# Block attention with the values and the softmax sums on four column tiles of TensorE, and its affine part on GpSimd

## The reference, cut to what matters

```python
q = split_heads(x @ Wq)          # 16 heads of 8 features
k = split_heads(x @ Wk)
v = split_heads(x @ Wv)
scores = jnp.einsum('bhqd,bhkd->bhqk', q, k) / jnp.sqrt(jnp.float32(HD))
attn_w = jax.nn.softmax(scores, axis=-1)
ctx = jnp.einsum('bhqk,bhkd->bhqd', attn_w, v)
ctx = ctx.transpose(0, 2, 1, 3).reshape(b, s, d)
attn_out = ctx @ Wo + bo
out1 = _layernorm(x + attn_out, ln1_g, ln1_b)
```

## Time and profile before

| | |
|---|---|
| median of three runs | 1562.96 us (1562.08 to 1563.18) |
| profiled execution, its own time | 1561.37 us |
| span of the profiled execution | 1559.6 us |
| PE busy | 1352.5 us (87%) |
| DVE busy | 845.7 us (54%) |
| ACT busy | 710.9 us (46%) |
| POOL busy | 146.7 us (9%) |
| the stage's first and last record | 1111.1 us and 1286.7 us |

### The profile page before, as it was taken

The page is one execution under the profiler, slowest core; times in us unless marked ns, Lnnn a source line. Parts: engine busy times, 40 slices in busy tenths (PEclk is TensorE's granted clock), DMA queues, the critical chain, the costliest instruction groups (busy, mean ns, idle before and its releaser), DMA issues. The chain is left out here.

```text
span 1559.6 us, 26943 instructions
## 1 busy us (share of the span) xinstructions
PE 1352.5 (87%) x8843; PEld 1045.2 (67%) x8843; DVE 845.7 (54%) x2280; ACT 710.9 (46%) x1593; POOL 146.7 (9%) x256
## 2 busy tenths in 40 slices
PE   6766799999996899689999997984699987999995
PEld 5642477777775487578888886973477764766664
DVE  4549777777763554645555553346687762122224
ACT  4331676776762302245555552442355542333343
POOL 1010000000001000000000002005244421000000
PEclk9869899999996999889999997995699987999998
DMA  8000000000000000000000004002000000000000
GB/s 335 1 1 0 1 1 1 1 1 2 1 1 1 1 1 0 1 1 1 2 1 2 1 1 115 8 1 108 1 1 1 0 1 1 1 1 1 1 1 28
DMA packets 6427, 24.52 MB, mean 16 GB/s; under 512 B 797, under 2 KB 1311, under 8 KB 5418
## 3 DMA queue, kind: packets, MB, share of 16 engines
q1 hardware_dynamic: 6314, 23.03, 4.3%
HBM read 21.98 MB, written 1.05 MB: 15 GB/s over the span
## 5 line engine op out<-in xcount | busy, mean ns | idle before, releaser
L1317 DVE SCALAR_TENSOR_TENSOR XN<-bank,gate,XN 128x128 f32<-128x128 f32 x256 | 89.8, 351 | 224.8 <-PE bank L1281 222.2
L1297 ACT ACTIVATE e_hidden<-bank,small 128x512 f32<-128x512 f32 x152 | 104.4, 687 | 214.6 <-PE bank L1269 214.5
L767 PE MATMUL bank<-a_va,a_pT 128*128 128x65 f32 x1024 | 129.4, 269 | 0.8 <-ACT a_pT L933 0.5
L1281 PEld LDWEIGHTS bank<-attention_weights,e_hidden 128*128 128x128 f32 x1024 | 119.2, 192 | 14.8 <-issue 14.8
L767 PEld LDWEIGHTS bank<-a_va,a_pT 128*128 128x128 f32 x1024 | 124.4, 192 | 2.3 <-ACT a_pT L933 0.8
L1019 DVE TENSOR_REDUCE a_mx<-bank 128x4 f32<-128x512 f32 x128 | 87.8, 686 | 64.9 <-PE bank L807 64.4
L1269 PE MATMUL bank<-XNT,attention_weights 128*128 128x512 f32 x256 | 121.2, 606 | 1.2 <-PEq L541 1.2
L1281 PE MATMUL bank<-attention_weights,e_hidden 128*128 128x128 f32 x1024 | 119.3, 275 | 0.0
L933 ACT ACTIVATE a_pT<-bank 128x512 f32<-128x512 f32 x128 | 76.6, 599 | 41.8 <-PE bank L840 41.8
L1027 DVE TENSOR_TENSOR a_shifted<-bank,a_mx 128x512 f32<-128x512 f32 x128 | 88.3, 690 | 3.4
L1912 PEld LDWEIGHTS bank<-blk_va,blk_pT 128*128 128x128 f32 x512 | 64.5, 194 | 33.5 <-issue 21.9
(11 more groups left out here) (353 smaller groups left out, 2646.3 us busy)
## 6 DMA issues: line engine op xcount, KB each, us to landing
attention_weights<-in_a SPq DMA_DIRECT2D x2, 2048.0 KB, 11.7
mod_ring<-in_mod_weights SPq DMA_DIRECT2D x4, 576.0 KB
ctx_both<-in_ctx SPq DMA_DIRECT2D x1, 2048.0 KB, 9.2
attention_weights<-in_up SPq DMA_DIRECT2D x1, 2048.0 KB, 8.2
attention_weights<-in_down SPq DMA_DIRECT2D x1, 2048.0 KB, 12.7
down<-in_down SPq DMA_DIRECT2D x1, 1536.0 KB, 18.2
down<-in_mod_weights SPq DMA_DIRECT2D x2, 576.0 KB
X<-in_x SPq DMA_DIRECT2D x4, 256.0 KB, 3.9
```

Source lines behind the costliest of these rows:

```text
L767: last = pe.matmul(value_bank[:, j * (W + 1):(j + 1) * (W + 1)], pT[:, i.slot(2), j * 128:(j + 1) * 128], va[:, p, g // 2 * 8 + 2 * j + g ...
L1281: last = pe.matmul(down_bank[j][:, 0:width], layer[0:rows, f, j * 128:(j + 1) * 128], down(g, f), start=f == 0, stop=f == NB - 1)
L1297: act.activation(hidden[0:rows, p, f, :], up_bank_of(i, f)[0:rows, :], function, bias=up_bias(g, f)).then_inc(hidden_ready, 1)
L1317: dve.scalar_tensor_tensor(out=total, in0=down_bank[j][:, e * D:(e + 1) * D], scalar=gate_column(k, 4 * q + j, g * per_group + e), in1=tot ...
```

## The change

Nine things change in `stage_block_attention`, and nothing outside it.

1. The values are computed turned. The weights are now 32 columns of `va` and the moving operand is `pT` of one head, 128 columns. Each of the four matmuls of an item lies on another column tile of the array (`tile_position=(0, 32 * c)`), and writes 32 partitions of one bank. `va` has a stride of 40 per head with zeros between, and the window that is loaded moves with the group, so that each item adds its four heads' rows in the right place: the bank accumulates over a batch's four items.
2. The softmax sums are four more such matmuls, with a matrix of ones and zeros as the weights, into a second bank.
3. A group of heads is now every fourth head (`own`).
4. VectorE's reciprocal covers 128 columns instead of 16, and its product is already the turned output `oT`. The transposition of line 1903 and ScalarE's copy of line 1974 go.
5. There is one value bank where there were two, so a batch's first values wait for the batch before (`o_normed`).
6. Scaling, shifting and the copy to `out1` move from VectorE to GpSimd, with the new lag `AFFINE`, behind `BLOCKS` in GpSimd's body.
7. `ADD`, `NORMALISE`, `TURN_OUT` and `KEEP` have a later lag by one, one, one and three.
8. The turned output lies in the projection's bank, so that `TURN_OUT` waits for `qkv_kept`, and a projection for `out_kept`.
9. All four programs are written out (`rolled=False`), and GpSimd clears all of `va` and `ones` first.

```diff
 
-    PROJECT, KEEP_QKV, BLOCKS, SCORE, EXP, TURN_P, VALUES, NORM_O, TURN_O, OUT, ADD, NORMALISE, KEEP, TURN_OUT = \
-        0, 1, 4, 3, 5, 5, 6, 6, 7, 7, 7, 8, 9, 10
+    PROJECT, KEEP_QKV, BLOCKS, SCORE, EXP, TURN_P, VALUES, NORM_O, OUT, ADD, NORMALISE, AFFINE, TURN_OUT, KEEP = \
+        0, 1, 4, 3, 5, 5, 6, 6, 7, 8, 9, 10, 11, 12
...
-        kD, va = sb("kD", [128, 2, H, S]), sb("va", [128, 2, H, W + 1])
+        kD, va = sb("kD", [128, 2, H, S]), sb("va", [128, 2, H * 40])
         shifted, probs, pT = sb("shifted", [128, 2, 512]), sb("probs", [128, 2, 512]), sb("pT", [128, 2, 512])
-        mx, rec = sb("mx", [128, 2, 4]), sb("rec", [128, H])
-        on, oT = sb("on", [128, D]), sb("oT", [128, D])
+        mx, rec = sb("mx", [128, 2, 4]), sb("rec", [128, S])
+        ones, oT, scaled = sb("ones", [128, 4 * 40]), sb("oT", [128, S]), sb("scaled", [128, 2, D])
...
-        score_bank, turn_bank, value_bank = k.ps[0:2], k.ps[2:4], k.ps[4:6]
-        project_bank, side_bank = k.ps[6], k.ps[7]
+        chain, scaled_ready, copied = sem("chain"), sem("scaled_ready"), sem("copied")
+        out_ready, out_turned, out_kept = sem("out_ready"), sem("out_turned"), sem("out_kept")
+        score_bank, turn_bank = k.ps[0:2], k.ps[2:4]
+        value_bank, sums_bank = k.ps[4], k.ps[5]
+        project_bank, y_bank = k.ps[6], k.ps[7][:, 0:128]
+        turned_out = project_bank[:, 384:512]
+        own = k.hmask.rearrange("p (c j) -> p j c", j=4)
         block = ctx.enter_context(nc.Block(no_gpsimd_drain=True))
 
         @block.gpsimd
         def _(pool):
-            pool.memset(va[:, :, :, W:W + 1], 1.0).then_inc(cleared, 1)
+            pool.memset(va[:, :, :], 0.0).then_inc(cleared, 1)
+            pool.memset(ones[:, :], 0.0).then_inc(cleared, 1)
+            pool.wait_ge(cleared, 2)
+            pool.memset(ones[:, :].rearrange("p (j w) -> p j w", w=40)[:, :, 0:W], 1.0).then_inc(cleared, 1)
 
             def body(at):
                 i = at(PROJECT)
@@ -1858,22 +1865,38 @@
                     if i.older_than(8):
                         await_count(pool, scored, i.number - 7)
                     pool.tensor_tensor(kD[:, p, 4 * g:4 * g + 4, :], kT[:, p, :].unsqueeze(1).to_broadcast([128, 4, S]),
-                                       k.hmask[:, 4 * g:4 * g + 4].unsqueeze(2).to_broadcast([128, 4, S]),
+                                       own[:, g, :].unsqueeze(2).to_broadcast([128, 4, S]),
                                        ALU.mult).then_inc(k_spread, 1)
-            sweep(pool, G, 8, TURN_OUT, body)
+                i = at(AFFINE)
+                if i.alive and i.offset % 4 == 3:
+                    b = batch_of(i)
+                    n, p = b.number, b.slot(2)
+                    await_count(pool, scaled_ready, n + 1)
+                    if b.older_than(2):
+                        await_count(pool, out_turned, n - 1)
+                        await_count(pool, copied, n - 1)
+                    pool.tensor_tensor(out[:, p, :], scaled[:, p, :], k.affine3(2), ALU.mult).then_inc(chain, 1)
+                    await_count(pool, chain, n + 1)
+                    pool.tensor_tensor(out[:, p, :], out[:, p, :], k.affine3(3), ALU.add).then_inc(out_ready, 1)
+                    await_count(pool, out_ready, n + 1)
+                    pool.tensor_copy(col(k.out1, n), out[:, p, :]).then_inc(copied, 1)
+            sweep(pool, G, 8, KEEP, body, rolled=False)
...
             def body(at):
                 i = at(TURN_OUT)
                 if i.alive and i.offset % 4 == 3:
                     b = batch_of(i)
                     await_count(pe, out_ready, b.number + 1)
-                    pe.transpose(side_bank[:, 256:384], out[:, b.slot(2), :], k.ident).then_inc(out_turned, 1)
+                    await_count(pe, qkv_kept, min(b.number + 4, B))
+                    if b.older_than(1):
+                        await_count(pe, out_kept, b.number)
+                    pe.transpose(turned_out, out[:, b.slot(2), :], k.ident).then_inc(out_turned, 1)
                 i = at(PROJECT)
                 if i.alive and i.offset % 4 == 0:
                     b = batch_of(i)
@@ -1881,6 +1904,8 @@
                     await_count(pe, staged, n + 1)
                     if b.older_than(1):
                         await_count(pe, qkv_kept, n)
+                    if b.older_than(4):
+                        await_count(pe, out_kept, n - 3)
...
-                i = at(TURN_O)
-                if i.alive and i.offset % 4 == 3:
-                    b = batch_of(i)
-                    await_count(pe, o_normed, b.number + 1)
-                    if b.older_than(1):
-                        await_count(pe, out_kept, b.number)
-                    pe.transpose(side_bank[:, 0:128], on[:, :], k.ident).then_inc(o_turned, 1)
                 i = at(VALUES)
                 if i.alive:
                     m, (b, g), p = i.number, i.part(4), (i.offset // 4) % 2
                     await_count(pe, p_kept, m + 1)
-                    if g == 0 and i.older_than(8):
-                        await_count(pe, o_normed, b - 1)
-                    for j in range(4):
-                        h = 4 * g + j
-                        last = pe.matmul(value_bank[p][:, h * (W + 1):(h + 1) * (W + 1)],
-                                         pT[:, i.slot(2), j * 128:(j + 1) * 128], va[:, p, h, :],
-                                         start=True, stop=True)
-                    last.then_inc(weighted, 1)
+                    if g == 0 and i.older_than(4):
+                        await_count(pe, o_normed, b)
+                    elif i.first:
+                        pe.wait_ge(cleared, 3)
+                    for bank, stationary, per_group in ((value_bank, va[:, p, :], 160), (sums_bank, ones[:, :], 0)):
+                        for c in range(4):
+                            first = c * per_group + 32 * g
+                            last = pe.matmul(bank[32 * c:32 * c + 32, 0:S],
+                                             stationary[:, first:first + 32], pT[:, i.slot(2), c * 128:(c + 1) * 128],
+                                             start=g == 0, stop=g == 3, tile_position=(0, 32 * c))
+                            if not per_group:
+                                last.then_inc(weighted, 1)
...
-                    await_count(pe, o_kept, b.number + 1)
-                    pe.matmul(side_bank[:, 128:256], oT[:, :], k.w3[:, 384:512], start=True,
+                    await_count(pe, o_normed, b.number + 1)
+                    if b.older_than(1):
+                        await_count(pe, added, b.number)
+                    pe.matmul(y_bank, oT[:, :], k.w3[:, 384:512], start=True,
                               stop=True).then_inc(y_done, 1)
-            sweep(pe, G, 8, TURN_OUT, body)
+            sweep(pe, G, 8, KEEP, body, rolled=False)
...
-                        await_count(act, weighted, 4 * n - 4)
+                        await_count(act, weighted, 16 * n - 16)
...
-                    act.activation(va[:, p, :, 0:W], project_bank[:, 256:384].rearrange("p (h w) -> p h w", w=W),
+                    act.activation(va[:, p, :].rearrange("p (h w) -> p h w", w=40)[:, :, 0:W], project_bank[:, 256:384].rearrange("p (h w) -> p h w", w=W),
...
-                i = at(TURN_O)
-                if i.alive and i.offset % 4 == 3:
-                    b = batch_of(i)
-                    await_count(act, o_turned, b.number + 1)
-                    if b.older_than(1):
-                        await_count(act, y_done, b.number)
-                    act.activation(oT[:, :], side_bank[:, 0:128], ACT.Copy).then_inc(o_kept, 1)
                 i = at(TURN_P)
                 if i.alive:
                     m, p = i.number, i.slot(2)
                     await_count(act, p_turned, m + 1)
                     if i.older_than(2):
-                        await_count(act, weighted, m - 1)
+                        await_count(act, weighted, 4 * m - 4)
                     act.activation(pT[:, p, :], turn_bank[p][:, :], ACT.Copy).then_inc(p_kept, 1)
-            sweep(act, G, 8, TURN_OUT, body)
+            sweep(act, G, 8, KEEP, body, rolled=False)
...
-                    dve.tensor_scalar(col(k.XNT, n), side_bank[:, 256:384], 1.0, None, ALU.mult).then_inc(out_kept, 1)
+                    dve.tensor_scalar(col(k.XNT, n), turned_out, 1.0, None, ALU.mult).then_inc(out_kept, 1)
                 i = at(NORMALISE)
                 if i.alive and i.offset % 4 == 3:
                     b = batch_of(i)
                     n, p = b.number, b.slot(2)
                     await_count(dve, rstd, n + 1)
-                    dve.tensor_scalar(r1[:, :], r1[:, :], stats[:, 6:7], stats[:, 7:8], ALU.subtract,
-                                      ALU.mult).then_inc(chain, 1)
-                    await_count(dve, chain, 3 * n + 1)
-                    dve.tensor_tensor(r1[:, :], r1[:, :], k.affine3(2), ALU.mult).then_inc(chain, 1)
```

(33 more changed lines are left out.)

## The result

The changed kernel takes 1606.1 us (median of four runs, 1605.13 to 1607.1) against 1562.5 (four runs, 1561.61 to 1563.18): a ratio of 1.0279, 95% interval 1.0262 to 1.0297, 43.6 us slower. The forecast was 1617. The profiled execution took 1606.18 us, with a span of 1604.4.

What follows compares the result with a forecast made beforehand. TensorE's instructions were taken to set the pace. Batches of 13.02 us against 10.16, with the ends, gave +43.1 us and the clock +10.5: +53.6 on 1561.4, 1615, so a median of 1617 us; range 1590 to 1670.

Steps and rivals of the forecast that it cites:

- The hold's chain: Once per batch, GpSimd waits for VectorE's `scaled_ready` between two `kD`, so the next scores wait: interval 4.80 us, about 2.3 before.
- S: Mark on TensorE: start of an item's second scores record, 0.43 us behind the first; intervals run from S to S.
- V: Time of an item's values on TensorE: 0.8 us on four column tiles, where 0.85 was taken before.
- the two-way row: Profile row of an earlier attention's scores: 16 records on two row tiles in 1.10 us, 0.2 of it entering and leaving.
- Column tiles do not overlap: Rival: the values' calls run serially on TensorE, V is 2.0 us, the kernel 1668 us; chance 0.19.
- `TURN_OUT` behind `qkv_kept`: The output's transposition on TensorE waits for ScalarE's Q, K, V copies: next S at x + 1.63 us instead of 1.01.
- The reciprocal: VectorE's reciprocal of 128 columns takes 1.01 us, hidden by 0.25; without TURN_OUT's wait it would show by 0.37.
- The clock: TensorE's granted clock falls in every second hold, 1.5 us each: +10.5 us, bounds 0 and 48.
- The rival of a fall that stays down for two stretches in every hold: Rival: TensorE's clock falls in every hold for two 3.4 us stretches: +91 us, 1654 us; chance 0.13.
- The ends: Outside items 9 to 61: items 61 to 63 +3.1 us, GpSimd's clearing at the start +1.3, last batch's end +0.5.
- Written-out programs: Writing out the stage's four programs gives 0.1 us a step at most, counted only through the intervals.
- The hidden hold: Rival: GpSimd's chain ends within an ordinary interval and V is 0.45: 9.06 us a batch, 1549 us; chance 0.04.

Runs made afterwards that it cites:

- u1_order: Changed kernel with the lag of AFFINE at 12 instead of 10, so GpSimd issues all four `kD` of a batch first: 1555.4 us, 0.9948 of before.
- u3_dummy: Changed kernel with 20 unused transpositions of the identity on TensorE once per batch, ahead of the held scores: 1592.6 us, 1.019 of before.
- v4_serial: Changed kernel with all eight value calls of an item on one column tile and a copy for the reciprocal (result lost): 1652.8 us, one run.
- v1_bank: Changed kernel, AFFINE still at 10, with the turned output in bank 7 instead of the projection's bank: 1600.6 us, 1.0238 of before.
- v2_cheap: u2_order_bank with a plain copy of the sums in place of the reciprocal (division left out): 1546.7 us, 0.9893 of before.
- u4_unrolled: The kernel before, with the four programs of the stage written out and nothing else: 1557.9 us, 0.9967 of before.
- u2_order_bank: Changed kernel with the lag of AFFINE at 12 and the turned output in bank 7, without TURN_OUT's wait for `qkv_kept`: 1548.5 us, 0.9906 of before.
- v3_pairs: Changed kernel with the value calls reordered, each column tile's values and sums calls one behind the other: 1607.1 us, one run.
- w1_clear: u2_order_bank with GpSimd clearing `va` and `ones` behind its first copy of the input instead of ahead of it: 1548.6 us, 0.9911 of before.

## Why the prediction was right

The direction and the mechanism held: the three GpSimd operations, queued in order between two `kD`, made a chain through three engines in each batch. u1_order shows it by moving them alone. Point by point, on the profiled executions (44.8 us apart; 53.6 forecast):

- *The hold's chain*, 4.80 forecast, 4.49 measured. GpSimd's operations were as taken (454 ns for 0.45; copy 0.29; `kD` 1.05). The 0.3 lies in small joints: the normalisation starts 0.60 after the maximum, not 0.74; from the copy to `kD` 0.25, not 0.32; from the weight load to S 0.43, not 0.54.
- *V*, 0.8 forecast, 0.58 measured: this was the mis-sized term. As an estimate it is four rounds of 0.11 and about 0.13 for entering and leaving the tiles, where the two-way row had given 0.2. The sum of the lower bound (0.65) was nearer than the value between the rows. In three intervals of a batch this is 0.22 too much each, of which 0.08, 0.15 and 0.06 were seen (2.78 for 2.86, 2.31 for 2.46, 2.84 for 2.90); the rest went to joints that the sum had left out, as the 0.52 from S to the values where it had 0.43. With the chain it makes 12.42 a batch for 13.02: from item 9 to 61 30.3 us for the 38.2 forecast, as u3_dummy's trace has it without a fall. The falls make it 43.0.
- *Column tiles do not overlap* (1668) fell. v4_serial shows what it would have been: 1.87 us a values step, 16.03 a batch, 1652.8 us. The sentence of the Trainium skill (TensorE: Matmul & The Clock Gate, Part 3), that weight loads overlap matmuls in flight only with another row group, does not hold here as the prediction read it: all eight calls share the rows, and they take 0.58 instead of 1.87 us once their columns differ.
- *`TURN_OUT` behind `qkv_kept`*, 0.62 forecast, 0.55 measured by v1_bank, and 0.15 more at the projection, which the forecast had not priced. (The copies take 0.62 in the earlier trace rows and not 0.64, which changes nothing.)
- *The reciprocal*, 1.01 forecast, 0.958 measured: (958 - 257) / 112 = 6.3 ns a column. Taking the repeat count of eight that the Trainium skill (VectorE: DVE Perf Modes, First, the fixed hardware budget) gives as eight cycles a column had led to an estimate 0.18 above the forecast. The trace is 0.05 below the forecast. It is hidden, as forecast. By the prediction it would show by 0.37 without `TURN_OUT`'s wait. In v2_cheap it was 0.09.
- *The clock*, +10.5 forecast (a fall in every second hold, 1.5 us each), 13.5 measured by u3_dummy: eleven falls in fourteen holds, about 1.2 us each (in the traces 12.7 up to item 61 and 1.6 behind it). The rival of a fall that stays down for two stretches in every hold had the falls nearly right; only one of them lasted so long.
- *The ends.* To the first scores it is +1.7 (1.3 forecast); the first nine items give 1.4 back (written out, with the shorter values, no hold yet); item 61 to 63 costs 3.9 with its fall (3.1); from the last scores to the stage's end it is 13.07 instead of 15.64, 2.6 less where 0.5 more was forecast. The three terms of the sum measured +0.7 for the reciprocal, -0.8 for the turn and the copy and +0.4 for GpSimd, near the +0.75, -0.9 and +0.6 forecast. What the sum left out is the last four values steps. They follow each other at 1.92 us where it was 2.1 to 2.8, so the last one starts 1.4 earlier. From there to the reciprocal it is 0.8 instead of 1.9. Most of that is the clock: it had fallen to 0.50 at 1277.2 in the kernel before, ahead of the last values, whose records took 1.88 us where those of the steps ahead took 0.95 to 1.15. Here it falls at 1328.9, behind them. With item 9 to 61 this is 43.0 + 1.7 - 1.4 + 3.9 - 2.6 = 44.6 of the 44.8.
- *Written-out programs* I counted "only through the intervals". u4_unrolled shows 0.39 us a batch in them, some 5 us in all. Whether the changed kernel has this gain too, under the hold, was not tried.
- *The hidden hold* (1549): its condition was one number of the lag line, and the kernel that it describes, with the shared bank, is u1_order: 1555.4 us and 9.85 a batch, where the prediction had 9.06. Its intervals were too short by 0.13 to 0.29 each, since it had V at 0.45. That u2_order_bank runs at 1548.5 is a coincidence, as the bank's gain makes up for that.

The total is nearer than its parts. Without the clock, the intervals up to item 61 came out 7.9 us under the forecast, items 61 to 63 0.8, the first nine items 1.4 and the end 3.1, and the start 0.4 over it. The clock took 3.8 more than forecast. The falls of the clock were a guess between bounds of 0 and 48, and that they offset part of the rest is luck.

## What to carry to other kernels

When work moves to an engine with time to spare, look at what already stands in its queue behind the new place and who waits for that: an engine that works through its queue in order and is idle for more than half of the time (GpSimd was busy for 71 of 173 us) sets the pace if a late input stops it just ahead of something urgent. Put the moved work behind the urgent one. Two steps of lag made 50 us here, for the same instructions. And a short idle time of TensorE costs more than its length where the clock falls after it; 2.3 us did that in eleven of fourteen holds, 1.0 us (v4_serial) in none.

## What the runs showed of the hardware

- TensorE's granted clock fell to 0.50 for 3.4 us after a pause of 2.3 us, in eleven of fourteen cases, and stayed at 1.00 when 20 useless transpositions (2.35 us) filled it. More work made the kernel 13.5 us faster. The length of the pause alone does not decide: at the end of the stage the kernel before had idled for 1.15 of 6.1 us when its clock fell (1277.2), and the changed kernel for 1.83 of 6.7 us (1318.94 to 1325.65) without a fall.
- Four column tiles: 16 records of 128 moving columns in 0.58 us against 1.87 on one tile. Calls on other column tiles start ahead of earlier ones whose tile is still busy (v3_pairs).
- A reciprocal of 128 fp32 columns takes 0.958 us, where a two-operand operation of GpSimd on as many takes 0.454.
- At a stage's start at half clock, 1.7 us gained ahead of the clock's rise left 0.9 us in the stage's trace, too little for the medians to show (w1_clear).
